# First block of a fused S4 / SwiGLU kernel: row tiles normalised one by one, shared between VectorE and ScalarE, with loads from two queues and moved folds

## The reference

```python
xn = _layernorm(x, axis=-1)                       # (x - mean) / sqrt(var + 1e-5)
s = S4(xn)                                        # causal convolution along the last axis, + D * xn
h1 = xn @ w1.T + 2 * (xn @ A1.T) @ B1.T           # LoRA on every linear layer
h3 = xn @ w3.T + 2 * (xn @ A3.T) @ B3.T
g  = silu(h1) * h3
x  = x + s * silu(g @ w2.T + 2 * (g @ A2.T) @ B2.T)
```

## Time and profile before

| what | value |
|---|---|
| median of 3 runs | 428.47 us |
| lowest, highest | 427.99, 428.89 us |
| the profiled execution's own time | 428.78 us |
| its span, first to last instruction | 427.0 us |
| PE busy | 419.1 us (98%) |
| DVE, ACT, POOL busy | 161.1, 102.6, 65.5 us |

### The profile page before, as it was taken

One profiled execution on the slowest core, in us unless ns is written; L12 is line 12 of the kernel. 1 busy time (PEld: TensorE's weight loads), 2 busy tenths in 40 slices (PEclk: granted clock), 3 DMA queues, 4 the chain that ended last, 5 costly groups with the idle time before them and its releaser, 6 DMA issues.

```text
span 427.0 us, 5022 instructions
## 1 busy us (share of the span) xinstructions
PE 419.1 (98%) x1868; PEld 341.2 (80%) x1868; DVE 161.1 (38%) x245; ACT 102.6 (24%) x168; POOL 65.5 (15%) x128
## 2 busy tenths in 40 slices
PE   8999999999999999999999999999999999999995
PEld 7977888887778888888788888888778888888773
DVE  4658586655486221224135222132324111111115
ACT  5543323333232111122112111212212111111111
POOL 3246725332050103200000101400000000000000
PEclk9999999999999999999999999999999999999999
DMA  8474822321315301000004301000002000000002
GB/s 266 118 222 128 310 81 73 89 81 31 97 66 178 118 2 50 2 0 0 2 22 149 124 0 50 0 0 0 0 0 99 0 0 0 0 0 0 0 0 98
DMA packets 14064, 26.19 MB, mean 61 GB/s; under 512 B 2481, under 2 KB 4209, under 8 KB 14033
## 3 DMA queue, kind: packets, MB, share of 16 engines
q1 hardware_dynamic: 13888, 25.41, 18.9%
q0 software_dynamic: 160, 0.59, 0.4%
HBM read 20.37 MB, written 4.53 MB: 58 GB/s over the span
## 4 chain that ended last, share of the span: by engine, by line
PE 95%; DVE 2%; DMA 1%; issue 1%; ACT 0%; SPq 0%; DVEq 0%; ACTq 0%
PE h L782 20%; PE h L783 20%; PE h L784 20%; PE f L784 9%; PE f L782 9%; PE f L783 9%; PE spare L769 2%; DMA lora_first<-lora_dram 1%; DVE w L625 1%; PE spare L764 1%; PE f L777 1%; PE spare L784 1%; PE spare L782 1%; PE spare L783 1%; DVE raw L615 0%
## 5 line engine op out<-in xcount | busy, mean ns | idle before, releaser
L782 PE MATMUL h<-xt,w 128*128 (+4 forms) x356 | 138.7, 390 | 0.2 <-DVE w L625 0.2
L784 PE MATMUL h<-xt,w 128*128 (+4 forms) x356 | 137.8, 387 | 0.0
L783 PE MATMUL h<-xt,w 128*128 (+4 forms) x356 | 137.8, 387 | 0.0
L782 PEld LDWEIGHTS h<-xt,w 128*128 128x128 f32 (+1 forms) x356 | 66.0, 185 | 15.9 <-DVE w L625 0.6
L784 PEld LDWEIGHTS h<-xt,w 128*128 128x128 f32 (+1 forms) x356 | 66.0, 185 | 14.9
L661 DVE TENSOR_TENSOR g<-g,h 128x512 f32<-128x512 f32 (+1 forms) x44 | 30.2, 687 | 126.1 <-PE h L784 126.1
L783 PEld LDWEIGHTS h<-xt,w 128*128 128x128 f32 (+1 forms) x356 | 66.0, 185 | 14.5
L666 DVE TENSOR_TENSOR ghl<-g,ghl 128x512 fp32r<-128x512 f32 (+1 forms) x44 | 32.0, 727 | 101.1 <-ACT ghl L521 101.0
L784 PE MATMUL f<-ghl,w2f 128*128 128x512 f32 (+1 forms) x176 | 69.5, 395 | 0.0
L782 PE MATMUL f<-ghl,w2f 128*128 128x512 f32 (+1 forms) x176 | 69.4, 395 | 0.0
L783 PE MATMUL f<-ghl,w2f 128*128 128x512 f32 (+1 forms) x176 | 69.2, 393 | 0.0
(11 more groups left out here) (103 smaller groups left out, 274.8 us busy)
## 6 DMA issues: line engine op xcount, KB each, us to landing
raw<-w_dram SPq DMA_DIRECT2D x28, 256.0 KB, 3.7
xres<-xT_dram SPq DMA_DIRECT2D x4, 1024.0 KB, 6.9
outT_dram<-xres SPq DMA_DIRECT2D x16, 256.0 KB, 2.4
rows_next<-x_dram SPq DMA_DIRECT2D x4, 512.0 KB, 3.7
scale_rows<-scales_scratch SPq DMA_DIRECT2D x3, 512.0 KB, 4.1
xn<-x_dram SPq DMA_DIRECT2D x4, 256.0 KB, 4.2
rows<-x_dram SPq DMA_DIRECT2D x2, 512.0 KB, 7.4
raw<-w_dram SPq DMA_DIRECT2D x4, 224.0 KB, 2.5
```

What stands on the lines that cost most here:

```text
L782: pe.matmul(out, w[1], m[0], start=start, stop=False)
L783: pe.matmul(out, w[0], m[1], start=False, stop=False)
L784: return pe.matmul(out, w[0], m[0], start=False, stop=stop)
```

## The change

Row tiles 0 and 1 are normalised by VectorE in one operation each (subtract the mean, multiply by the reciprocal deviation), tiles 2 and 3 by ScalarE as before, and every tile has its own statistics, epsilon (now on DVE) and power (POOL, one column) instead of a pair. Row tile 1 and `lora_first` are issued from ScalarE's queue. Fold (1, 0) stands ahead of the turning of tile 0, (3, 0) behind that of tile 1, (1, 1) ahead of that of tile 2; tile 3 is turned behind h3 for `lo`. The low part of fold (3, 0) goes to POOL. The fillers are 8, 1 and 1 instead of 7, 1 and 2.

```diff
-POOL_LO = [(3, 1), (1, 3), (3, 3), (3, 4)]
+POOL_LO = [(3, 0), (3, 1), (1, 3), (3, 3), (3, 4)]
...
             load_tile(0)
-            sync.dma_start(lr[:, :], lora).then_inc(lora_in, 16)
-            load_tile(1)
+            load_raw(1, 0)
             sync.dma_start(lane_c[:, :], lanes).then_inc(const_in, 16)
-            load_raw(1, 0)
             load_tile(2)
...
             def rows_norm(r):
-                act.wait_ge(shift_ready, r // 2 + 1)
+                act.wait_ge(first_shift, r - 1)
...
+            act.dma_start(xn[:, 1, :], x[P:2 * P, :]).then_inc(x_in[1], 16)
+            act.dma_start(lr[:, :], lora).then_inc(lora_in, 16)
...
-            rows_norm(0)
-            rows_norm(1)
-            fold_hi(1, 0)
             rows_hi(0)
             rows_hi(1)
+            fold_hi(1, 0)
+            fold_hi(3, 0)
             rows_norm(2)
+            rows_hi(2)
             rows_norm(3)
-            fold_hi(3, 0)
-            rows_hi(2)
             rows_hi(3)
             act.wait_ge(spread_in, 32)
             nc.scalar.copy(spread_hl[:, 0, :], spread[:, :]).then_inc(spread_hi, 1)
...
+            def rows_first(r):
+
+                rows_moments(0, r)
+                dve.wait_ge(moments_ready, r + 1)
+                nc.vector.tensor_scalar(scales[:, 0, r:r + 1], moments[:, r, 1:2], EPS, None, ALU.add) \
+                    .then_inc(first_eps, 1)
+
+            def rows_norm(r):
+
+                dve.wait_ge(first_rstd, r + 1)
+                nc.vector.tensor_scalar(xn[:, r, :], xn[:, r, :], moments[:, r, 0:1], scales[:, 0, r:r + 1],
+                                        ALU.subtract, ALU.mult).then_inc(xn_ready, 1)
...
-            rows_moments(0, 0)
-            rows_moments(0, 1)
-            rows_moments(0, 2)
+            rows_first(0)
+            rows_first(1)
+            rows_norm(0)
+            rows_norm(1)
             fold_add(1, 0)
-            rows_moments(0, 3)
-            fold_lo(1, 0)
             rows_lo(0)
             rows_lo(1)
+            fold_lo(1, 0)
+            rows_first(2)
             fold_add(3, 0)
-            fold_lo(3, 0)
+            rows_first(3)
+            fold_add(1, 1)
             rows_lo(2)
+            fold_lo(1, 1)
             rows_lo(3)
-            fold_add(1, 1)
-            fold_lo(1, 1)
             fold_add(3, 1)
...
-                keep_busy(7)
+                keep_busy(8)
                 pe.wait_ge(lora_in, 16)
                 fold(1, 0)
+                pe.wait_ge(const_in, 16)
+                turn_rows(0)
+                keep_busy(1)
+                turn_rows(1)
                 fold(3, 0)
                 keep_busy(1)
-                pe.wait_ge(const_in, 16)
-                turn_rows(0)
-                turn_rows(1)
-                keep_busy(2)
...
+                fold(1, 1)
                 turn_rows(2)
-                turn_rows(3)
                 wait_split(pe, 3, 0)
                 hidden(0, 0, 0, 3, h3, lo)
-                fold(1, 1)
+                turn_rows(3)
                 pe.wait_ge(xlo_done, RT)
...
+            nc.gpsimd.memset(half[:, :], -0.5).then_inc(half_set, 1)
+            pool.wait_ge(half_set, 1)
+            for r in range(RT):
+                pool.wait_ge(first_eps, r + 1)
+                tt(scales[:, 0, r:r + 1], scales[:, 0, r:r + 1], half[:, :], ALU.pow).then_inc(first_rstd, 1)
+                if r >= 2:
+                    pool.wait_ge(first_rstd, r + 1)
+                    nc.gpsimd.tensor_scalar(scales[:, 1, r:r + 1], moments[:, r, 0:1], scales[:, 0, r:r + 1], -1.0,
+                                            ALU.mult, ALU.mult).then_inc(first_shift, 1)
             pool.wait_ge(const_in, 16)
-            for r in range(0, RT, 2):
-                rows_rstd(0, r)
...
+            fold_lo(3, 0)
             pool.wait_ge(spread_hi, 1)
```

More of the change, by code:

```diff
@@ L237, in build @@
         small = put("small", [P, 4])
+        half = put("half", [P, 1])
         bvec = put("bvec", [P, 2])
@@ L306, in build @@
         eps_added, rstd_ready, shift_step, shift_ready = map(sem, ("eps_added", "rstd_ready", "shift_step", "shift_ready"))
+        first_rstd, first_shift = sem("first_rstd"), sem("first_shift")
+        first_eps, half_set = sem("first_eps"), sem("half_set")
         xn_ready, xt_turned = sem("xn_ready"), sem("xt_turned")
@@ L402, in spread_scales @@
             def spread_scales(b):
-                sync.wait_ge(shift_ready, (b + 1) * (RT // 2))
+                sync.wait_ge(shift_ready, b * (RT // 2))
                 sync.dma_start(scales_dram[:, :].rearrange("k (p r) -> p k r", r=RT), scales[:, :, :]) \
@@ L955, in rows_rstd @@
             def rows_rstd(b, r):
-                two, n = slice(r, r + 2), b * (RT // 2) + r // 2 + 1
+                two, n = slice(r, r + 2), (b - 1) * (RT // 2) + r // 2 + 1
                 pool.wait_ge(moments_ready, b * RT + r + 2)
@@ L1004, in _ @@
             tt(mag[:, :], mag[:, :], res[:, :], ALU.add).then_inc(mag_ready, 1)
-            for kind, j in POOL_LO[1:]:
+            for kind, j in POOL_LO[2:]:
                 fold_lo(kind, j)
```

## The result

The changed kernel takes **440.25 us** (median of four runs, 438.42 to 440.40) where the kernel before takes 428.68 us on the same chip: a ratio of 1.026, 95% interval 1.023 to 1.029. The prediction had 435.9 us in a range of 433.2 to 439.4. The direction is right, the loss is 11.6 us instead of 7.4, and the time lies above the range. The profiled execution took 440.4 us with a span of 438.6.

What follows compares the result with a forecast made beforehand. TensorE, busy 419.1 of 427.0 us, was taken as the bound. A 6.4 us later start of h1 for `hi` plus 1.0 us of clock made 7.4 us, giving a median of 435.9 us, range 433.2 to 439.4.

Steps and rivals of the forecast that it cites:

- the wait and its place: Behind turning 3: TensorE idle about 4 us until VectorE's L655; h1 for `hi` starts at 24.4, 6.4 us later.
- the loads: At the start: row tile 0 lands at 4.5 us, tile 1 at about 4.8, `lora_first` at 6.1.
- the normalisation: In the front: one VectorE normalisation of a row tile takes 0.45 us; TensorE wants tile 1 only at 9.4.
- the wait at h3 for `lo`: Ahead of turning 3: TensorE waits until 18.2 us for GpSimd's low part of fold (3, 0).
- the clock, both terms: Up to turning 3: a later clock rise costs 1.0 us, between nothing and 1.9; a fall in the wait was not summed.
- everything behind moves with TensorE: Behind the start of h1 for `hi`: all later work shifts by the same delay, with no further loss or gain counted.
- rival A: Clock falls in the wait behind turning 3: 2.2 us more lost, 438.1 us, up to 439.7; chance 0.25.
- Rival B: Clock rises during the eight opening fillers: folds and turnings take half, clock term gone, 433.4 us; chance 0.09.
- Rival C: Not slower: the front comes forward by as much as the uncovered hand-over costs, about 428 us; chance 0.04.

Runs made afterwards that it cites:

- d1: Kernel before with VectorE's list alone changed: fold_add and low part of fold (1, 1) ahead of row tile 3's low part; 438.23 us, ratio 1.022.
- d2: Changed kernel with ScalarE's cast of fold (1, 1) ahead of that of `lora_spread`; 436.97 us.
- a1: Changed kernel with row tile 3's low part ahead of fold (1, 1)'s in VectorE's list; 433.37 us.
- a4: Changed kernel with all loads back on SyncE's one queue in the old order; 440.41 us.
- a2: Changed kernel with sixteen unread filler matmuls between turning 3 and h1 for `hi`; 434.43 us.
- f1: d1 with eleven unread matmuls in TensorE's wait behind fold (1, 1); 431.38 us.
- c2: Kernel before with nine fillers instead of seven at the start and eight instead of one behind fold (3, 0); 428.61 us.
- a3: Changed kernel with its second half put back as before on TensorE, VectorE and ScalarE, the new front kept; 429.70 us.
- b1: Changed kernel with old second half, fold (3, 0)'s low part on VectorE, `lora_first` on SyncE's queue, earlier statistics of tiles 2 and 3, nine opening fillers; 430.06 us.
- b3: b1 with all row tiles normalised by ScalarE, tile 3's statistics behind fold (1, 0)'s low part, and more fillers in TensorE's gaps; 428.86 us.
- c1: Kernel before with nine fillers instead of seven at the start; 429.00 us.

## Why the prediction was right or wrong

**Right: the wait and its place.** The forecast had TensorE idle for about 4 us behind turning 3, released by VectorE's L655. It is 4.31 us. The chain under it came link by link: ScalarE's three casts 1.79 us (forecast 2.0 with hand-overs), VectorE's L626 at 1.81 us, ending 0.54 us after GpSimd's subtraction (forecast 0.55 from the earlier trace rows), tile 3's low part 0.61. d1 shows that VectorE's order alone opens such a wait and costs 9.4 us in the kernel before, d2 that the stretch is GpSimd's, and a1 that the old order takes 2.9 us off the wait.

**Right: the loads.** `lora_first` landed at 6.30 (forecast 6.1), and TensorE's folds began at 6.34 (6.15). Row tiles 0 and 1 landed at about 3.9 and 4.1, both earlier than the 4.5 and 4.8 of the forecast; TensorE waited for `lora_first` either way. The rule cited there, from the Trainium skill (DMA: Bandwidth & Descriptors, Issuing engines are not separate DMA queues), is not contradicted: with one queue (a4) the time is 440.41, with two 440.25, and a4's runs spread over 4.5 us.

**Right in size, of no weight: the normalisation.** I took 0.45 us; L650 takes 0.54 and 0.55. The estimate of 0.42 from the Trainium skill (VectorE: DVE Perf Modes, The perf-mode tier table) is further off, and its working was not shown: a quarter of the 1.23 us for 2048 columns would be 0.31. The measured duration stands. TensorE asks for tile 1 only at 9.88, two microseconds after it is there.

**Not seen: the wait at h3 for `lo`.** GpSimd's low part of fold (3, 0) ended at 18.01, forecast 18.2. TensorE came only at 19.07, made late by its own clock. In a2, where the clock was up, that wait is there (17.98). The step was right under the clock it assumed.

**Wrong: the clock, both terms.** In front I took 1.0 us, the middle between nothing and 1.9. (The bound used 0.24 us for a matmul at half clock and elsewhere 0.28; they are 0.21 apart, so it was somewhat high.) h1 for `hi` started at 26.06, not 24.4, and a2, with the clock up ahead of h3 for `lo`, puts it at 24.46: the term is 1.6, inside its bounds. The step that failed is the sentence that "everything behind moves with TensorE", with the clock's fall in the wait left to rival A at 0.25 and a price of 2.2 us. In every profiled execution with an unfilled wait of 2.5 us or more here, the clock was at its lower level behind it (the changed kernel, a4, d1, d2; in a4 ahead of it too), and f1, with the same wait filled, kept it up. So the fall belonged in the sum. And the price was 3.8 in the changed kernel and 6.2 in d1, not 2.2. That price rested on 4.4 us of work before the rise at 13.6 us in the kernel before; from 26.06 the clock was back only at 34.4 us. Even rival A, as priced, ended at 439.7, below the 440.25 measured. With 1.6 in place of 1.0 and 3.8 in place of 0, the forecast's 7.4 becomes 11.8, where 11.6 was measured. The rule from the Trainium skill that I named for rival A (TensorE: Matmul & The Clock Gate, Part 1), idleness brings the half clock back, agrees with this trace: 0.50 from 25 to 30 us behind 4.31 idle us. It does not account for c2, where the clock fell with TensorE at work.

**Rival B** (the clock rises during the eight fillers) did not occur in the profiled execution: the folds took 2.07 us for eight records, half clock. In a1, a3 and d2, whose lists on TensorE are the same up to there, they took 1.15: the clock had risen, and it fell again at about 8 us. So B's first step comes and goes from one execution to the next, but the gain that was priced with it did not follow, since the clock didn't stay. **Rival C** (not slower) is excluded by the result, and in a3, b1 and b3, with the second half repaired, the front still wins nothing.

What stays open: why the same list raises the clock early in one execution and not in another; what sets how long it stays down behind a wait (some 8 us in the changed kernel, 13.5 in d1, 7 in d2); and what makes it fall at about 8 us. There it fell during waits of 1.7 and 2.1 us (d1, c1) but also without one (c2), so these waits can't be called the cause. All these fronts have 16-row folds ahead of the fall, and no kernel without them was tried. The folds alone do not bring it down later on: in the kernel before, fold (1, 1) at 16.99 passes at full speed.

## What to carry to other kernels

When a change opens a wait in front of the engine that bounds the kernel, price it twice: its length, and what the clock then costs on the work behind it. Here 2.8 us of waiting cost 6.2 more, and unread matmuls in the wait gave that back. Filling comes second, though: order each supporting engine's list by who is waited for next. Row tile 3's low part was the next thing TensorE needed, and one fold's low part with the cast behind which it stood was put ahead of it. And ask what the supporting chain allows before buying clock or earlier inputs in front: with TensorE at full speed from about 6 us on, b3 began h1 for `hi` no earlier.

## What the runs showed of the hardware that was not expected

- The clock falls late. Behind waits of 2.8 us (d1) and 2.5 us (d2) the first matmuls still ran at full speed, 0.12 us apart, for about 0.5 and 0.7 us; only then came 0.21. In the changed kernel the clock fell 2.4 us into a wait of 4.3 us, and the matmuls behind it are 0.21 us apart at once.
- It can fall without a wait: in c2 at 8.2 us, with TensorE at work since 5.41, first on 16-row folds and then on 128-row fillers.
- It can stay down through uninterrupted work: in d1 from 21.7 to 35.2 us with TensorE busy without a gap.
- The granted clock column does not show the level of the first stretch. It prints 1.00 for the first 13 us of the kernel before, where eight transposes take 1.71 us instead of 0.87; after a fall it prints 0.50. In the first stretch only the spacing of equal matmuls tells.
- VectorE's subtraction for fold (1, 1), with two operands in SBUF, took 1.81 us beside GpSimd's and ended 0.54 us after it. In d2, done before GpSimd began, it took 0.69. Row tile 3's low part, which reads a bank that TensorE wrote, took 0.68 in d2 beside GpSimd's operation: no stretch.
